# A two-FFN and attention layer on one core: layernorm rows written by ScalarE, and the router's steps moved into three slots

## The reference, cut to what matters

```python
def _layernorm(x, axis=-1, eps=1e-05):
    return (x - mean) / sqrt(var + eps)

def ffn(x):                                  # 8 experts, K = 2
    probs = softmax(x @ router_w.T)          # tokens x 8
    top_w, top_idx = top_k(probs, 2)
    top_w = top_w / (sum(top_w) + 1e-09)
    h = relu(x @ w1[e].T + b1[e])            # 512 hidden channels per expert
    y = h @ w2[e].T + b2[e]
    return sum of the two chosen y, weighted by top_w

x = x + 0.5 * ffn(_layernorm(x))
x = x + attention(_layernorm(x))
x = x + 0.5 * ffn(_layernorm(x))
```

## Time and profile before

| what | us |
|---|---|
| median of 3 runs | 518.18 (518.05 to 520.53) |
| the profiled execution, its own time | 518.44 |
| its span, first to last instruction | 516.6 |
| TensorE busy | 486.4 |
| VectorE busy | 373.3 |
| ScalarE busy | 287.3 |
| GpSimd busy | 222.2 |

### The profile page before, as it was taken

One profiled execution on the slowest core, in us unless ns is written; L12 is line 12 of the kernel. 1 busy time (PEld: TensorE's weight loads), 2 busy tenths in 40 slices (PEclk: granted clock), 3 DMA queues, 4 the chain that ended last, 5 costly groups with the idle time before them and its releaser, 6 DMA issues.

```text
span 516.6 us, 5885 instructions
## 1 busy us (share of the span) xinstructions
PE 486.4 (94%) x1782; PEld 288.8 (56%) x1782; DVE 373.3 (72%) x704; ACT 287.3 (56%) x447; POOL 222.2 (43%) x228
## 2 busy tenths in 40 slices
PE   7999999999999999999988968999996999999996
PEld 3566675565455446554644634555562545677774
DVE  3555188759958699995977799857869984666443
ACT  2766587654346565344557423357752435587873
POOL 0034320649951245884024358811517882113222
PEclk9999999999999999999999999999999999999999
DMA  7191111074310017710003625111054411003100
GB/s 226 55 369 47 41 42 41 3 223 162 105 41 1 1 41 186 243 62 1 1 0 128 200 82 158 48 62 41 0 145 144 153 71 41 0 1 124 63 0 20
DMA packets 20575, 43.52 MB, mean 84 GB/s; under 512 B 3776, under 2 KB 3904, under 8 KB 20544
## 3 DMA queue, kind: packets, MB, share of 16 engines
q1 hardware_dynamic: 14208, 31.61, 18.8%
q10 hardware_dynamic: 6336, 11.54, 7.1%
HBM read 39.86 MB, written 3.28 MB: 83 GB/s over the span
## 4 chain that ended last, share of the span: by engine, by line
PE 54%; issue 18%; POOL 13%; DVE 12%; ACT 2%; POOLq 0%; DVEq 0%; ACTq 0%
PE Y L316 17%; PE U L295 7%; PE U L297 7%; PE U L296 7%; POOL xT L809 5%; POOL qs L825 5%; PE Y L311 2%; PE Y L313 2%; PE Y L312 2%; DVE hid_lo L680 2%; PE A L385 2%; DVE pool_a L733 2%; POOL carry L822 2%; POOL pool_a L831 1%; DVE xnt L615 1%
## 5 line engine op out<-in xcount | busy, mean ns | idle before, releaser
L501 ACT ACTIVATE hid<-U,small 128x512 f32<-128x512 f32 x188 | 128.7, 687 | 157.9 <-PE U L297 145.2
L316 PE MATMUL Y<-hid,w 128*128 128x512 f32 x376 | 191.8, 591 | 0.0
L809 POOL TENSOR_TENSOR xT<-xT,gy 128x512 f32<-128x512 f32 x64 | 87.1, 1360 | 213.2 <-DVE gy L689 213.1
L295 PE MATMUL U<-xhi,w1lo 128*128 128x512 f32 x256 | 168.2, 657 | 7.7 <-ACT hid L501 6.6
L297 PE MATMUL U<-xhi,w1hi 128*128 128x512 f32 x256 | 101.1, 395 | 0.0
L296 PE MATMUL U<-xlo,w1hi 128*128 128x512 f32 x256 | 100.3, 392 | 0.0
L825 POOL TENSOR_TENSOR qs<-q,pool_a 128x512 f32<-128x512 f32 x64 | 82.3, 1285 | 21.8 <-DVE pool_a L716 21.8
L295 PEld LDWEIGHTS U<-xhi,w1lo 128*128 128x128 f32 x256 | 48.3, 189 | 74.7 <-issue 56.5
L316 PEld LDWEIGHTS Y<-hid,w 128*128 128x128 f32 x376 | 70.8, 188 | 16.1
L680 DVE TENSOR_TENSOR hid_lo<-hid,hid_hi 128x512 fp32r<-128x512 f32 x68 | 52.6, 780 | 26.8 <-ACT hid_hi L499 26.5
L296 PEld LDWEIGHTS U<-xlo,w1hi 128*128 128x128 f32 x256 | 48.6, 190 | 38.7 <-issue 36.9
(11 more groups left out here) (122 smaller groups left out, 469.0 us busy)
## 6 DMA issues: line engine op xcount, KB each, us to landing
G<-gate_dram SPq DMA_DIRECT2D x32, 512.0 KB, 4.0
vb<-v_dram ACTq DMA_DIRECT2D x44, 256.0 KB, 3.3
vb<-v_dram SPq DMA_DIRECT2D x20, 256.0 KB, 4.3
pool_a<-wexp_dram SPq DMA_DIRECT2D x8, 256.0 KB, 7.0
w<-wexp_dram SPq DMA_DIRECT2D x8, 256.0 KB, 7.1
v_dram<-v SPq DMA_DIRECT2D x8, 256.0 KB, 2.2
xT<-xT_dram SPq DMA_DIRECT2D x4, 256.0 KB, 7.9
out_dram<-xT SPq DMA_DIRECT2D x4, 256.0 KB, 2.8
```

Source lines behind the costliest of these rows:

```text
L295: mm(dst, w1lo[:, e, f, :], xhi[:, k % NB, :], start=True, stop=False)
L316: mm(dst, w2[:, g % E, f, :], hid[:, n % HS, :], start=first, stop=final).then_inc(down, 1)
L501: act.activation(hid[:, n % HS, :], U[n % 2][:, :], ACT.Relu, bias=bias).then_inc(h_f, 1)
L809: pool.tensor_tensor(xT[:, h, b, :], xT[:, h, b, :], gy[:, g % 2, :], ALU.add).then_inc(acc, 1)
```

## The change

Three things are altered.

1. VectorE's normalise becomes scales(): 1/std as before, then one 128x4 operation, shift = -mean/std. The four passes over the rows are done by ScalarE as ACTIVATE Identity with scale 1/std and bias shift, in the same slot t = 2; a new semaphore ln_rst leads from VectorE to ScalarE.
2. The factor 0.5 moves into the last product of step 4, and the operation that made 0.5/sum (L670) goes. Steps 1 to 5 are done in three slots: (1, 2), (3, 4), (5).
3. gates_to_rows(k) and the earliest slot of gates_in(k, c) come two slots earlier, at PREP[k] + T_RT + 3.

```diff
@@ gates_slot
-    return max(4 * (k * E + (c + 1) * EQ - GS) + 4, PREP[k] + T_RT + 5 if k else 0)
+    return max(4 * (k * E + (c + 1) * EQ - GS) + 4, PREP[k] + T_RT + 3 if k else 0)
@@ sync
-                    if n == PREP[k] + T_RT + 5:
+                    if n == PREP[k] + T_RT + 3:
                         gates_to_rows(k)
@@ scalar
+            def normalise(ln, bank):
+                act.wait_ge(ln_rst, ln + 1)
+                for t in range(4):
+                    at = ln % 2 * 4 + t
+                    last = act.activation(xnt[:, at, :], bank[:, t * P:(t + 1) * P], ACT.Identity,
+                                          bias=shift[:, at:at + 1], scale=rstd[:, at:at + 1])
+                last.then_inc(ln_nrm, 1)
+
...
+                if t == T_NRM:
+                    normalise(LN_FFN[k], A[3])
...
+                if t == T_NRM:
+                    normalise(LN_ATT[i], A[0])
...
             split_w1(0)
+            normalise(0, A[0])
             ffn_hi(0, A[0])
@@ vector
-            def normalise(ln, bank):
+            def scales(ln):
                 dve.wait_ge(ln_std, ln + 1)
-                t0 = ln % 2 * 4
-                link(dve.reciprocal(rstd[:, t0:t0 + 4], std[:, t0:t0 + 4]))
-                for t in range(4):
-                    last = dve.tensor_scalar(xnt[:, t0 + t, :], bank[:, t * P:(t + 1) * P],
-                                             mv[:, t0 + t, 0:1], rstd[:, t0 + t:t0 + t + 1], ALU.subtract, ALU.mult)
-                last.then_inc(ln_nrm, 1)
+                v = slice(ln % 2 * 4, ln % 2 * 4 + 4)
+                link(dve.reciprocal(rstd[:, v], std[:, v]))
+                dve.scalar_tensor_tensor(out=shift[:, v], in0=mv[:, v, 0], scalar=-1.0, in1=rstd[:, v],
+                                         op0=ALU.mult, op1=ALU.mult).then_inc(ln_rst, 1)
...
-                    link(dve.tensor_tensor(m(3), m(7), m(2), ALU.mult))
+                    link(dve.scalar_tensor_tensor(out=flat(m(3)), in0=flat(m(7)), scalar=0.5, in1=flat(m(2)),
+                                                  op0=ALU.mult, op1=ALU.mult))
...
-                    link(dve.tensor_scalar(r(5), r(7), 0.5, None, ALU.mult))
-                    link(dve.tensor_tensor(gate[:, b].rearrange("p e t -> p t e"), m(3), bc(r(5)), ALU.mult))
+                    link(dve.tensor_tensor(gate[:, b].rearrange("p e t -> p t e"), m(3), bc(r(7)), ALU.mult))
...
-                if T_RT <= t < T_RT + 5:
-                    route(k, t - T_RT + 1)
+                if T_RT <= t < T_RT + 3:
+                    for step in ((1, 2), (3, 4), (5,))[t - T_RT]:
+                        route(k, step)
```

More of the change, by code:

```diff
@@ L128, in program @@
         rstd = sb("rstd", [P, 8])
+        shift = sb("shift", [P, 8])
         epsc = sb("epsc", [P, 1])
@@ L178, in program @@
         w1hi_s, w1lo_s, rw_r, setup, out_done = sem("w1hi_s"), sem("w1lo_s"), sem("rw_r"), sem("setup"), sem("out_done")
-        ln_src, ln_var, ln_std, ln_nrm, ln_T = (sem(n) for n in ("ln_src", "ln_var", "ln_std", "ln_nrm", "ln_T"))
+        ln_src, ln_var, ln_std, ln_rst, ln_nrm, ln_T = (sem(n) for n in ("ln_src", "ln_var", "ln_std", "ln_rst", "ln_nrm", "ln_T"))
         xn_hi, xn_lo, xa_rdy = sem("xn_hi"), sem("xn_lo"), sem("xa_rdy")
@@ L695, in prepare @@
                 if t == T_NRM:
-                    normalise(LN_FFN[k], A[3])
+                    scales(LN_FFN[k])
                 if t == T_LO:
@@ L723, in attend @@
                 if t == T_NRM:
-                    normalise(LN_ATT[i], A[0])
+                    scales(LN_ATT[i])
                 if t == T_XM:
@@ L777, in _ @@
             dve.tensor_tensor(rwh[:, 1, :], w(W_RT, E), rwh[:, 0, :], ALU.subtract).then_inc(rw_r, 1)
-            normalise(0, A[0])
+            scales(0)
             split_w1(0)
```

## The result

| | median us | runs |
|---|---|---|
| before | 518.36 (518.03 to 520.66) | 10 |
| changed | 522.31 (520.67 to 523.27) | 10 |

The ratio is 1.0058, with a 95% interval from 1.0042 to 1.0074: about 3 us slower. The medians are 3.9 us apart, since six of the ten executions of the kernel before lie at 518.0 to 518.5 us and four at 520.3 to 520.7. I had said 516.3 us. The profiled execution took 523.0 us, with a span of 521.0. Lines of the changed kernel are 1 higher than before on TensorE and SP, 9 on ScalarE's ACTIVATEs of hid and 12 or 13 on VectorE and GpSimd: L298 is L297 of before, L721 and L729 are L708 and L716, L701 is L689, L780 is L767.

What follows compares the result with a forecast made beforehand. TensorE, busy 94% of the span, was taken as the bound, with waits traced partly to VectorE's lateness. Terms 0.4 + 0.9 + 2.3 - 3.9 - 1.6 - 0.1 = -2.0 us gave 516.3 us, range 511.8 to 521.2.

Steps and rivals of the forecast that it cites:

- Head, +0.4: At the head, the chain std, scales, xnt, transposes has nothing beside it, so ScalarE's xnt costs 0.4 us.
- Unit 0, +0.9: Layernorms at slots 36 and 39: two times 1.6 us on busy ScalarE delay relus; +0.9 us, between 0 and 3.2.
- short idle times behind 75.6 take some of it, and a relu has up to a slot in hand: Unit 0: why ScalarE's two added 1.6 us would make up(39) only 0.45 us late and up(44) 0.9.
- Unit 1, +2.3: Unit 1 as a whole: v and vb wait behind G in SP's queue, delaying scan 0; +2.3 us, between -1.5 and +4.
- 0.7 to 0.9 us are gained: Unit 1, slots 81 to 86: lighter VectorE removes TensorE's 1.55 us wait; 0.7 to 0.9 us gained as far as slot 86.
- v lands at about 197.3: Unit 1's v, issued at 191.7 behind two G loads, lands at 197.3 instead of 193.5; scan 0 starts at 201.1.
- Unit 2, -3.9: No steps between unit 2's first scans, -3.7; slot 127 costs +0.9, won back at slot 133; -3.9 us, between -2 and -4.8.
- the clock is no term: Whole kernel: the granted clock is full in all 40 slices, so no cost was given to it.
- Unit 3, -1.6: Block 6's step 5 no longer stands between scans 0 and 1; -1.6 us, between -0.8 and -2.5.
- Rival 3: ScalarE becomes the bound: relus fall behind; unit 0 costs 3.2, unit 1 +4, total +4.1, 522.5 us; 13%.
- my sign for it: Sign that the forecast is wrong: ScalarE waits over 1 us for scales() in more than two places.
- Rival 1: Unit 1's v is not held up in SP's queue: unit 1 counts about -0.9, total -5.2, 513.2 us; 27%.

Runs made afterwards that it cites:

- e10: The changed kernel with the layernorms of block 2 and unit 0 (slots 36 and 39) given back to VectorE; 520.41 us, 1.0026 of the kernel before.
- e4: The changed kernel with gate rows and loads of G back in their old slot, PREP+T_RT+5; 517.87 us, 0.9975 of the kernel before.
- e2: The kernel before with only the routing change: five steps in three slots, the factor 0.5 folded in; 514.94 us, 0.9917 of the kernel before.
- e9: e8 with ScalarE writing the normalised rows of block 3 and unit 1 alone, and shift allocated last; 509.61 us, 0.9820 of the kernel before.
- e11: The changed kernel with ScalarE's four xnt one slot later (T_NRM + 1); 522.10 us, 1.0054 of the kernel before.
- e7: The changed kernel with gate rows still early but the loads of G issued in PREP+T_RT+5, behind v; 518.09 us, 0.9977 of the kernel before.
- e5: The changed kernel with the 32-byte tile shift allocated last, so other tiles keep their old addresses; 520.92 us, 1.0044 of the kernel before.
- e3: The kernel before with the routing change and the earlier gate rows and G loads, VectorE still normalising; 518.64 us, 0.9992 of the kernel before.
- e8: e2 with block 4's steps of slots 127 to 129 behind attend() on VectorE; 510.92 us, 0.9846 of the kernel before.
- e1: The kernel before with only the normalised rows moved to ScalarE; 522.09 us, 1.0066 of the kernel before.
- e6: The kernel before with an unused tile of 32 bytes per partition in shift's place; 520.19 us, 1.0014 of the kernel before.
- e12: The kernel before, five steps in five slots, with only block 4's steps behind attend() on VectorE; 517.44 us, 0.9967 of the kernel before.

## Why the prediction was wrong, point by point

1. **Head, +0.4.** It showed +0.7, but a head differs by up to 0.8 us from kernel to kernel. Nothing to learn from it.
2. **Unit 0, +0.9.** It came to +2.5 (slots 26 to 47), of which 2.1 are edit 1's (e10, and e4 against e2), 0.3 edit 2's (slot 44 in e2) and 0.1 the address. The step that failed is "short idle times behind 75.6 take some of it, and a relu has up to a slot in hand": I counted two times 1.6 us of engine time, and not the 1.55 us for which ScalarE stands ahead of the second xnt. My upper bound of 3.2 held it. The rule of the Trainium skill that I set beside this edit (ScalarE: Activation LUTs, Rules for kernel authors), to leave multiplications and additions to VectorE, is borne out in its sign by edit 1 as a whole, 3.0 to 3.4 us, but not at every place: in e9 ScalarE writes two of the layernorms, and the ledger gains 1.2 us by them. Some 1.3 us of edit 1's cost are the tile's address. How much of the rest is engine time and how much the wait for shift, e11 does not settle.
3. **Unit 1, +2.3.** It came to +3.2. "0.7 to 0.9 us are gained" up to slot 86: 1.3, the wait for o is gone. Then the chain through SP and the queue, in the order drawn, +4.2 at slots 99 to 104. G was issued at 194.21 and v at 195.07; my 191 and 191.7 did not hold the 3.2 us by which all was late by then. "v lands at about 197.3", 5.6 us after its issue, was 6.6. The mechanism was right (e7), its size 0.9 us short.
4. **Unit 2, -3.9.** It came to -1.4 (slots 127 to 147), and here my sum failed most. The scans closed up by 3.7, as written, though the first started 0.5 us later against its slot, so that 3.2 show. Slot 128's wait grew from 1.60 to 2.48, the 0.9 I had; at slot 133 1.8 came back, twice what I had said. What I left out stands in the first paragraph of the prediction: "the granted clock is full in all 40 slices, so the clock is no term". In the profiled execution it was one, +1.6 (changed against e5, which has the same wait without the fall). One full profile also says nothing of the other executions. A fall takes 0.003 off an execution's mean granted clock, and one in its last microseconds takes off nearly as much although nothing is left to lose there (e7 has one 2.7 us before its end). At 0.996 or less, which such a fall at the end does not make alone, are 8 of the changed kernel's 10 executions and 10 of the 73 of the kernel before that were timed with the experiments; at 0.997 or less they are 9 and 37. So the change made falls more frequent, and the kernel before is not always free of them. And slots 134 and 135 cost another 1.1 us in the changed kernel, e4, e5, e7 and e10, which have edit 1 there, and nothing in e2, e3 and e8, which have not: ScalarE waits 2.92 us for shift at 281.63 and has relus and tanh behind it. It needs edit 2 beside it: e1 shows nothing at these two slots, but its wait at slot 133 has not shrunk. I had set ScalarE's part in unit 2 to zero.
5. **Unit 3, -1.6.** It came to -1.5. A fall of the clock at slot 188 costs 1.6 us, and the stall of 1.4 at slot 202, which the kernels without this fall have, is then missing: the scans set the end there, not TensorE.
6. **A term I did not have at all:** +1.3 us from the address of the new tile (e5, e6), 0.9 of it outside the stretches above.

Together 0.3 (head) + 1.6 + 0.9 + 2.5 + 0.1 + 0.9 = 6.3 us, from -2.0 to the ledger's +4.3. Each stretch missed to the same side: most of it are costs that I had judged covered, and the address I had not thought of.

Rival 3, "ScalarE becomes the bound", gave 522.5 us, and the time was 522.31. It is not what happened. It came near the time by luck. It priced unit 1 at +4 for relus, where edit 1 gained 1.3 and SP's queue took 4.2, and with edit 1 but without edit 3 the kernel is faster than before (e4). Its part on unit 0 is right at 2.1 of the 3.2 us, and my sign for it came true: ScalarE waits over 1 us for shift in three places (1.55, 1.94 and 2.92 us). Rival 1 was e7's kernel in effect; in it unit 1 (slots 83 to 104) counts -0.9, but the total is 518.1, not 513.2, for the reasons of points 2, 4 and 6. The low end of my range, 511.8, does not follow from its own terms, which give 512.1 to 512.3; it changes nothing here.

## What to carry to other kernels

A move in a hand-written order has to be followed in every queue that it passes: loads of G issued two slots earlier cost 4 us through a DMA queue that hands out in order, and the same steps ahead of one xT cost 4 us through a wait and the clock behind it. A full granted clock in one profile does not say that other executions of the same kernel have it; where a change lengthens a wait of TensorE, price the wait and a fall behind it (here 1.6 us in the executions that have it). Put a new small tile behind the others, and compare the length of undisturbed slots before looking for a cause among the engines.

## What the hardware showed that I had not expected

- **The clock falls at waits of 2.5 us, but not always.** TensorE stood still for 2.48 to 2.51 us, ahead of the state products of slot 128 (L404 before) or, in e1, of the transposes of xnt, in nine profiled executions: the changed kernel, e1 to e5, e7, e10 and e11. The granted clock went to 0.50 in six of them, from 0.3 us before the end of the wait (e1) to 1.1 us after it (the changed kernel), and stayed at 1.00 in e3, e5 and e10. Two shorter waits close together also brought it (1.29 and 1.90 in the changed kernel, 1.28 and 1.89 in e2, 1.25 and 1.90 in e12), or did not (1.29 and 1.90 in e4, 1.24 and 1.90 in the kernel before). What decides is not shown by these runs. Each fall lasted 3.4 us, the one after three waits in e12 6.8; a fall of 3.4 us cost TensorE some 1.4 to 1.6. e5 at the same place as above, full clock:

```profile
267.00:268.00 1.00, 0.00 (x0) 0.00 (x0) 0.86 (x5) 0.10 (x1) 0.11 (x1) 1.00 0.00 0
268.00:269.00 1.00, 0.00 (x0) 0.00 (x0) 0.93 (x4) 0.00 (x0) 0.00 (x0) 1.00 0.00 0
...
270.00:271.00 1.00, 1.00 (x3) 0.14 (x2) 0.87 (x4) 0.60 (x1) 0.00 (x0) 1.00 0.00 0
271.00:272.00 1.00, 1.00 (x5) 0.72 (x5) 0.90 (x5) 0.59 (x1) 0.00 (x0) 1.00 0.02 8
```

- **It also goes with a spread of the runs.** e2's six executions took 513.67 and 513.72 us at a mean granted clock of 0.999 or more, and 514.75 to 515.26 at 0.992 to 0.996. The kernel before has it too: in the rounds of e1 to e4, ten of its 23 executions were at 1.000, 518.12 to 518.67 us, and the other 13, at 0.994 to 0.998, 517.54 to 520.56. The 520.53 among the three times given at the start may be such an execution; its clock is not on record. The clock is not the whole of the spread: e6's seven executions at 1.000 took 518.42 to 520.19 us.
- **32 bytes of SBUF cost 10 ns a product.** The second first-layer product goes from 390 to 400 ns and the slot from 1.547 to 1.560 us when the tiles behind it are shifted by 32 bytes per partition.
